# Folds of the key and query weights moved one or two places later in a fused decoder layer on one Trainium2 core

## What is computed

```python
x = x + self_attention(layernorm(x))          # 16 heads of 16, rotary, per-head layernorm on q and k, softmax
x = x + cross_attention(layernorm(x), ctx)    # 16 heads, latent width 64 for the context
x = x + experts(layernorm(x))                 # 8 experts, best 2 of each token
```

```python
q_big = rope((h @ Wq.T).reshape(B, S, H, K) @ w_kc_q)   # 192 wide for each head
q_r = q_big @ W_qr
k_r = rope(ctx) @ W_kr
scores = q_r @ k_r.T
```

## Time and profile before

| | |
|---|---|
| median of 3 runs | 671.04 us (670.31 to 672.01) |
| the profiled execution | 671.66 us |
| its span in the profile | 669.8 us |
| PE busy | 599.4 us (89%) |
| DVE busy | 494.1 us (74%) |
| ACT busy | 336.5 us (50%) |
| chain of waits, by engine | PE 67%, DVE 16%, ACT 9%, issue 5% |

### The profile page before, as it was taken

How to read it: one execution, slowest core, us unless ns; L and a number is a source line. 1 busy time by engine, 2 the same in 40 slices (tenths; PEclk the granted TensorE clock), 3 DMA queues, 4 the chain that set the end, 5 groups by cost and what they waited for, 6 DMA issues and landing times.

```text
span 669.8 us, 14896 instructions
## 1 busy us (share of the span) xinstructions
PE 599.4 (89%) x5522; PEld 454.1 (68%) x5522; DVE 494.1 (74%) x1173; ACT 336.5 (50%) x1175; POOL 251.2 (37%) x228
## 2 busy tenths in 40 slices
PE   2787989998899999999999999999987889799990
PEld 1556777777778766776777766777655578688880
DVE  4899799998366797737987389874885876555567
ACT  1377999999572024741157212670336844355550
POOL 2104000000003853833457834766445513643432
PEclk9897999998799999999999999999997999799996
DMA  8699990000000000000000120002036113333376
GB/s 288 174 337 342 325 319 8 2 2 1 1 2 17 17 0 3 2 1 17 1 2 2 64 64 1 2 9 94 12 107 210 49 48 95 113 110 110 98 258 212
DMA packets 40583, 58.96 MB, mean 88 GB/s; under 512 B 14944, under 2 KB 35040, under 8 KB 39872
## 3 DMA queue, kind: packets, MB, share of 16 engines
q1 hardware_dynamic: 34096, 45.94, 22.3%
q0 software_dynamic: 3408, 9.34, 3.8%
q10 hardware_dynamic: 3008, 2.72, 1.3%
HBM read 46.56 MB, written 29.40 MB: 113 GB/s over the span
## 4 chain that ended last, share of the span: by engine, by line
PE 67%; DVE 16%; ACT 9%; issue 5%; DMA 1%; another core or an unknown queue 1%; ACTq 0%; DVEq 0%
PE bank L395 58%; PE bank L404 9%; ACT ex L1675 2%; DVE x L1574 2%; ACT kbd L1665 2%; DVE nmax L1082 1%; DMA lncol<-in_L_attn_ln_kv_b 1%; DVE wlo L1507 1%; DVE m L1181 1%; ACT ex L1785 1%; DVE yr L1044 1%; DVE hvar L1049 1%; DVE newton L1065 1%; ACT xth L1631 1%
## 5 line engine op out<-in xcount | busy, mean ns | idle before, releaser
L1946 POOL TENSOR_TENSOR r<-m,m 128x512 f32<-128x512 f32 x80 | 104.4, 1328 | 102.1 <-DVE m L1181 87.7
L1181 DVE TENSOR_TENSOR m<-bank,cst 128x512 f32<-128x512 f32 x192 | 121.8, 683 | 24.5 <-PE bank L395 20.1
L1785 ACT ACTIVATE ex<-bank,nmax 128x64 f32<-128x64 f32 x256 | 73.1, 337 | 24.3 <-DVE nmax L1473 24.3
L395 PE MATMUL bank<-xth,wbh 128*128 128x512 f32 x192 | 79.9, 416 | 0.0
L395 PE MATMUL bank<-xth,wbl 128*128 128x512 f32 x192 | 75.2, 392 | 0.0
L395 PE MATMUL bank<-xtl,wbh 128*128 128x512 f32 x192 | 75.0, 390 | 0.0
L1768 ACT ACTIVATE qc<-bank 128x512 f32<-128x512 f32 x32 | 17.4, 595 | 101.8 <-PE bank L395 101.8
L395 PE MATMUL bank<-wop,qc 128*128 128x256 f32 x256 | 62.1, 388 | 0.0
L1993 POOL DMA_INDIRECT results<-ys,place x39 | 37.6, 965 | 62.2 <-ACT ys L1857 57.9
L395 PEld LDWEIGHTS bank<-wop,qc 128*128 128x128 f32 x256 | 46.4, 190 | 13.6 <-issue 7.2
L1675 ACT ACTIVATE ex<-bank,nmax 128x64 f32<-128x64 f32 x256 | 54.3, 357 | 2.5 <-DVE nmax L1082 2.4
(11 more groups left out here) (241 smaller groups left out, 1426.9 us busy)
## 6 DMA issues: line engine op xcount, KB each, us to landing
slots<-in_fill SPq DMA_DIRECT2D x1, 17544.0 KB, 65.3
xs<-slots SPq DMA_DIRECT2D x39, 129.0 KB
gb<-results SPq DMA_DIRECT2D x6, 512.0 KB, 4.7
wo_s<-in_L_xattn_Wo SPq DMA_DIRECT2D x1, 2048.0 KB, 18.1
wq_s<-in_L_xattn_Wq SPq DMA_DIRECT2D x1, 2048.0 KB, 11.8
wraw<-in_L_ffn_Wg SPq DMA_DIRECT2D x8, 256.0 KB, 3.8
wraw<-in_L_ffn_Wu SPq DMA_DIRECT2D x8, 256.0 KB, 4.1
wraw<-in_L_ffn_Wd SPq DMA_DIRECT2D x8, 256.0 KB, 4.8
```

The costliest lines, as they stand in the source:

```text
L395: return e.matmul(o, l, r, start=start, stop=stop, skip_group_check=True)
L1181: last = e.tensor_tensor(m4[n % 2][m][:, :].rearrange("p (b s) -> p b s", s=S), products[half][:, :].rearrange("p (b s) -> p b s", s=S), t ...
L1785: last = e.activation(ex[b % 4][:, h * 64:(h + 1) * 64], score_banks(b)[odd][:, n * 64:(n + 1) * 64], ACT.Exp, bias=nmax[b % 4][:, 4 * odd ...
L1946: last = e.tensor_tensor(rope[n % 6][half][:, :], m4[n % 2][first][:, :], m4[n % 2][second][:, :], op)
```

## The change

Only numbers in `ONCE` change, so only the order of steps. The key folds 0 and 1 go from 184.08 and 189.42 to 188.6 and 192.3, their copies likewise; the query folds 3 and 4 go from 205.86 and 210.3 to 208.36 and 211.5, their ACT and DVE steps by as much.

```diff
-    "kTe": [...], "wk": [184.08, 189.42, 223.36],
-    "wke": [184.98, 190.32, 224.26], "oT": [...],
+    "kTe": [...], "wk": [188.6, 192.3, 223.36],
+    "wke": [189.5, 193.2, 224.26], "oT": [...],
...
-    "qf0": [198.07, 200.34, 202.25, 205.86, 210.3, 213.22, 219.87, 221.87], ...
+    "qf0": [198.07, 200.34, 202.25, 208.36, 211.50, 213.22, 219.87, 221.87], ...
```

More of the change, by code:

```diff
@@ L122 @@
     "out_bias": [50.77], "borow": [51.77], "kcol": [40], "kT": [71.74, 89.78, 111.42, 115.23, 117.4, 136.24, 138.86, 157.51, 179.95, 182.43],
-    "kTe": [72.34, 90.38, 112.02, 115.83, 118, 136.84, 139.46, 158.11, 180.55, 183.03], "wk": [184.08, 189.42, 223.36],
-    "wke": [184.98, 190.32, 224.26], "oT": [21.34, 27.84, 31.02, 32.47, 35.98, 37.9, 38.76, 42.08],
+    "kTe": [72.34, 90.38, 112.02, 115.83, 118, 136.84, 139.46, 158.11, 180.55, 183.03], "wk": [188.6, 192.3, 223.36],
+    "wke": [189.5, 193.2, 224.26], "oT": [21.34, 27.84, 31.02, 32.47, 35.98, 37.9, 38.76, 42.08],
     "oTe": [21.99, 28.49, 31.67, 33.12, 36.63, 38.55, 39.41, 42.73], "wp": [30.69, 34.11, 39.16, 48.95], "wpe": [31.39, 34.81, 39.86, 49.65],
[3 rows of a table removed]
[3 rows of a table added]
     "fns": [197.5], "fpow": [197.5], "fnx": [210.74], "fnT": [215.65, 222.75], "fnh": [216.15, 223.25], "fnl": [216.65, 223.75],
```

## The result

| | before | changed |
|---|---|---|
| median, 20 runs each | 671.0 us (666.86 to 672.01) | 672.85 us (670.3 to 676.33) |
| ratio | | 1.003, 95% interval 1.0018 to 1.0042 |
| the profiled execution | 671.66 us | 670.42 us |
| its span | 669.8 us | 668.6 us |
| PE busy | 599.4 us (89%) | 597.2 us (89%) |

The changed kernel is slower by 0.3%, 2.0 us (1.2 to 2.8). Its profiled execution is one of its fastest, 2.4 us under its own median, and even under that of before. 1.94 us of that stand ahead of the change: the last key transposes start at 157.86 us where before has 159.80. So the two traces can't be compared by their ends; they are compared from one mark to the next inside the stretch that the change touches.

What follows compares the result with a forecast made beforehand. PE was taken to bound the kernel, busy 89% of the span and without idle behind the change. Key folds +0.9 and query folds +1.45 gave +2.35 us on the median 671.04, so 673.4 us; range 671.0 to 675.6.

Steps and rivals of the forecast that it cites:

- second place: Query folds 3 to 5, near 188 to 198 us: new waits ahead of S1 and fold 5's halves, +1.45 us (1.0 to 1.9).
- first place: Key folds 0 and 1, near 160 to 176 us: the wait for E0 loses its cover, +0.9 us (-0.6 to +1.9).
- The cost is handed to the end: PE behind the change has no idle, so time lost near 160 to 200 us is lost at the end, microsecond for microsecond.
- bound of +0.5 at full clock: Key folds, if PE ran at full clock throughout: wo would end about 0.5 us later than before.
- Rivals 1 and 3: Key folds, clock falling later: near 162.3 to 164 us, +1.9 us, chance 0.15; or near 165.4, -0.6 us, chance 0.21.
- Rival 2: Query folds: frequent small idles bring the clock down there too, +1.7 us more, 675.1 us in all; chance 0.08.
- Rival 4: Key folds: anT splits the idle and the clock does not fall, -4.5 us there, 668.0 us in all; chance 0.06.

Runs made afterwards that it cites:

- both fillings: Kernel before plus useless matmuls in PE's two long idles, 7 ahead of key fold 0 and 4 ahead of query fold 1; ratio to before 0.9893.
- query folds alone: Kernel before with only query folds 3 and 4 and their ACT and DVE steps moved; ratio to before 1.0026, +1.7 us (0.8 to 2.7).
- undoing the softening move: Kernel before with query fold 4 alone moved, fold 3's high parts staying ahead of E1; ratio to before 1.0023, +1.5 us (0.7 to 2.5).
- high part ahead of C1: Changed kernel with one number changed, so query fold 4's second high part precedes C1 on ACT; ratio to before 1.0012, +0.8 us (-0.2 to 1.8).
- key folds alone: Kernel before with only key folds 0 and 1 and their copies moved; ratio to before 1.0007, +0.5 us (-0.5 to +1.3).
- two kernels: Kernel before with only the key folds moved, and the changed kernel, each with 4, 6 and 4 useless matmuls in long idles; ratios to before 0.9911 and 0.9937.
- fillings hold the clock: Changed kernel plus useless matmuls, 4 ahead of anT, 6 between anT and T0, 4 ahead of query fold 1; ratio to before 0.9937.

## Why the prediction was right

The forecast was 673.4 us, +2.35 over the median; the measured median is 672.85, and the measured difference 2.0 us (1.2 to 2.8). The term of the second place holds by each of its steps. That the sum came so close is in part luck: the term of the first place can't be told from zero in the timed runs, and with zero there the sum would have been +1.45, which the measured interval takes in as well.

- **The cost is handed to the end.** Right as far as the runs can tell. PE is busy for 60.00 of 60 us behind the place in the trace after too, but that row was too little for "no idle at all": from 500 us on the trace before has PE busy for 137.52 of 170. The large change shows it best: with both fillings B is 7.15 us shorter, and from the last key transposes to the end of the span it is 7.19 (502.81 against 510.00). The small ones scatter: B and C of the changed kernel add up to +1.28, and to the end it is +0.74. Timed, C's 1.34 us came out as 1.7 (0.8 to 2.7) with the query folds alone.
- **Second place, +1.45.** Right by each step: idle ahead of `S1` 1.05 expected, 0.98 found; ahead of fold 5's halves 0.3 and 0.7 expected, 0.15 and 0.59 found, with `wbh` behind `ssb` on ACT as the cause; C +1.34. In the traces, taking the wait away with one number gave back 0.84, and undoing the softening move cost 0.78 more.
- **First place, +0.9.** Right in its waits; its size hangs on the clock, and the 0.9 is not shown. The trace arithmetic said +0.67 for the end of `wo`. In the one trace in which the clock rose only as `wo` ended (high part ahead of C1) A shows +0.71. In the changed kernel A shows +0.22: the clock rose while `wo` was running, so that `wo` took 3.06 us from start to start (170.72 to 173.78) instead of 3.58, which is the 0.5. The second stretch at half clock then lay partly over idle (it fell at 180.1, while PE waited until 180.54), and B ended level with before. The prediction raised 0.67 to 0.9 because a moved fall would be a later one; in the changed kernel and with the key folds alone it was earlier, 1.74 and 1.62 us behind the last key transposes against 2.16. Timed, the key folds cost +0.5 (-0.5 to +1.3). With the clock held up, A is +0.9 in two kernels. The bound of +0.5 at full clock that the prediction gave was too low: it let `S1` begin 6.3 us behind the last key transposes in the kernel before, where the filled trace has 6.15, and it had no wait for the copy of fold 1 ahead of `wo`, which is 0.20. `S1` came 7.0 us behind the last key transposes (164.86 against 157.86), as forecast (166.7 against 159.80 is 6.9).
- **Rivals 1 and 3, a later fall in the first place** (+1.9 and -0.6): neither came in the changed kernel, whose fall was earlier. The later one of the trace above, at 2.72 us, left A at +0.71. No trace of a kernel with both key folds moved and no fillings shows +1.9 or -0.6.
- **Rival 2, a fall of the clock in the second place** by what the Trainium skill says of small idles ("TensorE: Matmul & The Clock Gate", "A second HAM failure mode: psum-queue depth-cycling"): did not come. With 0.27, 0.98, 0.15 and 0.59 us of idle within 9 us the rows show 1.00; the measurement decides for this pattern.
- **Rival 4, the clock not falling at all** because `anT` splits the idle: the change did not do that. Its price for this place, -4.5 us against before, is near what the changed kernel shows when fillings hold the clock: A 11.08 against 15.70.
- **The chances.** Slower by over 0.3% had 0.54 and the same 0.40; the result lies on that line.

## What to carry to other kernels

When a piece of work is moved out of a wait, ask which wait it covered and what stands in its place; with the clock held up, a fold of 1.08 us behind the idle that it used to fill made the place 0.9 us longer. A copy that waits for another engine should not stand between two halves of something that a third engine is waiting for. Before fine moves of 1 us, look at the granted clock: an idle of 1.8 us on TensorE cost some 7 here through the half clock that followed, and matmuls without use, put into it, gave these back.

## What was not expected of the hardware

Filling 1.8 us of idle with 7 useless matmuls (1.9 us of PE) saved 6.9 us of 671, since the clock stayed at 2.4 GHz over work that had stood at 1.2 GHz for 13.7 us, and over a second such stretch of 3.4 us. The same idle of 1.62 us was followed by half clock in one kernel's trace and by full clock in another's. And one kernel took 671 us on two sets' chips and 663.5 on the third's, 1.1% apart, almost four times the effect under study. Why was not looked into.
